# Attention scores and outputs on one core: three 16-column products per block added in PSUM, in place of two products and an addition on VectorE

## The reference

```python
qkv = x @ qkv_w.T + qkv_b
q, k, v = (...)                                   # 12 heads of 16 channels
attn = jnp.einsum('bhid,bhjd->bhij', q, k) * scale
a = jax.nn.softmax(attn, axis=-1)                 # the first layer masks attn before this
out = jnp.einsum('bhij,bhjd->bhid', a, v)
return out @ out_w.T + out_b
```

## Time and profile before

| What | Value |
|---|---|
| Runs before | 509.74, 505.12 and 509.55 us, median 509.55 |
| The profiled execution | 506.86 us, span 505.1 us, mean granted TensorE clock 0.780 |
| PE busy | 344.7 us (68%), 3474 matmuls |
| PEld busy | 257.1 us (51%), 3474 weight loads |
| DVE busy | 412.2 us (82%), 896 instructions |
| ACT busy | 227.3 us (45%), 391 instructions |
| POOL busy | 144.7 us (29%), 194 instructions |

### The profile page before, as it was taken

How to read it: one execution, slowest core, us unless ns; L and a number is a source line. 1 busy time by engine, 2 the same in 40 slices (tenths; PEclk the granted TensorE clock), 3 DMA queues, 4 the chain that set the end, 5 groups by cost and what they waited for, 6 DMA issues and landing times.

```text
span 505.1 us, 8830 instructions
## 1 busy us (share of the span) xinstructions
PE 344.7 (68%) x3474; PEld 257.1 (51%) x3474; DVE 412.2 (82%) x896; ACT 227.3 (45%) x391; POOL 144.7 (29%) x194
## 2 busy tenths in 40 slices
PE   4766649897769899999926000006799268798976
PEld 4665619596646567776702000004359125655955
DVE  3799998998886654887779999998899869776974
ACT  4566383718375796644315660000084122363171
POOL 3535252042430433242042469811301120000000
PEclk9979986959577999999968555555599668578586
DMA  7635000030050002000000000000000000000000
GB/s 275 228 106 228 2 1 1 1 143 1 2 215 1 2 0 95 2 1 1 0 2 1 0 0 0 0 1 0 2 0 1 1 1 1 1 2 1 2 34 31
DMA packets 4235, 17.51 MB, mean 35 GB/s; under 512 B 857, under 2 KB 1762, under 8 KB 3682
## 3 DMA queue, kind: packets, MB, share of 16 engines
q1 hardware_dynamic: 4194, 16.95, 9.2%
HBM read 16.16 MB, written 0.79 MB: 34 GB/s over the span
## 4 chain that ended last, share of the span: by engine, by line
DVE 46%; PE 34%; ACT 8%; issue 6%; POOL 4%; DMA 1%; SPq 0%; DVEq 0%; POOLq 0%; ACTq 0%
PE PS L1527 30%; DVE R L1108 4%; DVE R L1378 3%; DVE R L1380 3%; POOL rstd L511 3%; DVE R L1432 2%; DVE Q L1098 2%; PE PS L1659 2%; DVE R L1001 1%; DVE stats L1011 1%; DMA T<-tok_w 1%; DVE xn L1021 1%; DVE stats L964 1%; POOL ve L508 1%; PE PS L1666 1%
## 5 line engine op out<-in xcount | busy, mean ns | idle before, releaser
L1527 PE MATMUL PS<-late_a,Q 128*128 128x192 f16 x48 | 9.9, 360 | 72.0 <-DVE Q L1435 70.3
L508 POOL TENSOR_SCALAR ve<-mv 128x1 f32<-128x1 f32 x56 | 14.4, 257 | 149.9 <-DVE mv L1012 131.1
L1527 PE MATMUL PS<-Q,R 128*128 128x32 f16 (+3 forms) x1024 | 46.4, 192 | 14.0 <-DVE R L1108 9.7
L1527 PE MATMUL PS<-m,Q 128*128 128x192 f16 (+1 forms) x576 | 51.9, 245 | 2.4 <-DVE Q L1324 2.4
L1527 PEld LDWEIGHTS PS<-Q,R 64*64 64x64 f16 (+1 forms) x1024 | 44.6, 125 | 17.2 <-DVE R L1108 10.2
L1527 PEld LDWEIGHTS PS<-m,Q 128*128 128x128 f16 (+1 forms) x576 | 45.8, 96 | 11.8 <-issue 8.0
L1527 PEld LDWEIGHTS PS<-late_a,Q 128*128 128x128 f16 x48 | 6.2, 139 | 73.8 <-issue 73.4
L1324 DVE TENSOR_TENSOR Q<-Q 128x512 f16<-128x512 f32 x36 | 26.5, 751 | 19.2 <-ACT Q L813 19.0
L1527 PE MATMUL PS<-X_hi,R 128*128 128x512 f16 x144 | 41.2, 392 | 0.0
L808 ACT ACTIVATE Q<-PS,col 128x512 f32<-128x512 f32 x36 | 24.8, 689 | 28.9 <-PE PS L1527 28.8
L1108 DVE TENSOR_SCALAR R<-Q,K 128x1024 f16<-128x1024 f16 x80 | 37.3, 539 | 0.3
(11 more groups left out here) (233 smaller groups left out, 932.3 us busy)
## 6 DMA issues: line engine op xcount, KB each, us to landing
R<-tok_x SPq DMA_DIRECT2D x8, 480.0 KB, 3.6
T<-tok_w SPq DMA_DIRECT2D x6, 480.0 KB, 7.3
T<-late SPq DMA_DIRECT2D x1, 2632.0 KB, 8.7
T<-moe SPq DMA_DIRECT2D x1, 2304.0 KB, 8.8
T<-moe SPq DMA_DIRECT2D x1, 1728.0 KB, 8.0
T<-full SPq DMA_DIRECT2D x1, 1152.0 KB, 5.3
R<-early SPq DMA_DIRECT2D x1, 776.0 KB, 9.8
out<-H SPq DMA_DIRECT2D x4, 192.0 KB, 1.9
```

What stands on the lines that cost most here:

```text
L508: nc.gpsimd.tensor_scalar(ve[:, t:t + 1], mv[:, t, 1:2], EPS, None, ALU.add).then_inc(pool_step, 1)
L1527: return T_.matmul(o, w, x, start=start, stop=stop, skip_group_check=True)
```

## The change

A block's three products now go to the same 16 columns, one after the other, and add in PSUM: high weights by high tokens, high weights by low tokens, low weights by high tokens. VectorE's additions are gone. A fill holds 16 sequences instead of 8, so a stage fills two banks instead of four; within a fill, first all blocks of 128 rows are computed, then all of 64. Scores are copied out of PSUM by ScalarE (two copies of 128x512 in a stage) instead of being written by VectorE. Outputs are split straight from PSUM by ScalarE and VectorE.

```diff
-                for i in range(4 if step in ("st", "ot") else 2):
-                    f.add((step, a, hf, i), by={"st": "st_ready", "pt": "pt_ready", "ot": "os_ready"}.get(step))
+                for i in range(2):
+                    f.add((step, a, hf, i), by={"st": "st_ready", "pt": "pt_ready", "ot": "ot_ready"}.get(step))
...
-                    elif step in ("pt", "ot"):
+                    elif step in ("st", "pt", "ot"):
                         for pr in range(2):
...
+                            name = (step, a, hf, pr)
+                            filled(name)
+                            v = bank(name).rearrange("p (t k n) -> p t k n", t=2, k=2)
+                            if step == "st":
+                                nc.scalar.activation(ST[:, pr], v, ACT.Copy).then_inc(st_ready, 1)
                             else:
-                                act.wait_ge(os_ready, 4 * (2 * a + hf) + 2 * pr + 2)
-                                d, v = O_hi, OS[:, 2 * pr:2 * pr + 2]
...
+                                d = PT[:, 0] if step == "pt" else O_hi
+                                d = d[:, 2 * pr:2 * pr + 2]
+                                nc.scalar.activation(d[:, :, 0], v[:, :, 0], ACT.Copy).then_inc(act_step, 1)
+                                ast[0] += 1
+                                nc.scalar.activation(d[0:CB, :, 1], v[0:CB, :, 1], ACT.Copy).then_inc(hi_ready, 1)
...
-                def two_columns(dst, src):
-                    return V.tensor_reduce(dst, src.rearrange("p (l n) -> p n l", l=2), AX, ALU.add)
-
-                def scores_sum(hf):
-
-                    if 2 * a + hf:
-                        dve.wait_ge(ot_ready, 2 * (2 * a + hf))
-                    for i in range(4):
-                        name = ("st", a, hf, i)
-                        filled(name)
-                        b = bank(name)
-                        two_columns(ST[:, i // 2, i % 2, 0], b[:, 0:2 * P])
-                        two_columns(ST[0:CB, i // 2, i % 2, 1], b[0:CB, 2 * P:4 * P]).then_inc(st_ready, 1)
...
                 def outputs_low(hf):
 
-                    for i in range(4):
-                        name = ("ot", a, hf, i)
-                        filled(name)
-                        b = bank(name)
-                        two_columns(OS[:, i, 0], b[:, 0:2 * P])
-                        two_columns(OS[0:CB, i, 1], b[0:CB, 2 * P:4 * P]).then_inc(os_ready, 1)
                     for pr in range(2):
+                        name = ("ot", a, hf, pr)
                         next_high()
+                        v = bank(name).rearrange("p (t k n) -> p t k n", t=2, k=2)
                         sl = slice(2 * pr, 2 * pr + 2)
-                        V.tensor_tensor(O_lo[:, sl], OS[:, sl, 0], O_hi[:, sl, 0], ALU.subtract)
...
+                        V.tensor_tensor(O_lo[:, sl], v[:, :, 0], O_hi[:, sl, 0], ALU.subtract)
...
-                    for t in range(4):
-                        name = ("st", a, hf, t)
+                    for pr in range(2):
+                        name = ("st", a, hf, pr)
                         free(name)
-                        oa, ob = (bank(name)[:, 2 * P * k:2 * P * (k + 1)].rearrange("p (l n) -> p l n", l=2) for k in range(2))
-                        for s in range(8):
-                            g = 8 * t + s
-                            q, o = slice(16 * g, 16 * g + 16), slice(16 * s, 16 * s + 16)
-                            mm(oa[:, :, o], KAbd[:, 0, g], qa[:, :, q], True, False)
-                            mm(oa[:, 0, o], KAbd[:, 1, g], qa[:, 0, q], False, True)
...
+                        o = bank(name).rearrange("p (t k s n) -> p t k s n", t=2, k=2, s=8)
+                        for kd, qd, k, m in ((KAbd, qa, 0, P), (KVBbd, qb, 1, CB)):
+                            for g in range(16 * pr, 16 * pr + 16):
+                                d, q = o[0:m, g // 8 % 2, k, g % 8], slice(16 * g, 16 * g + 16)
+                                mm(d, kd[0:m, 0, g], qd[0:m, 0, q], True, False)
+                                mm(d, kd[0:m, 0, g], qd[0:m, 1, q], False, False)
+                                last = mm(d, kd[0:m, 1, g], qd[0:m, 0, q], False, True)
                         last.then_inc(psum_filled, 1)
...
-                        pe.wait_ge(st_ready, 4 * (2 * a + hf) + 2 * pr + 2)
+                        pe.wait_ge(st_ready, 2 * (2 * a + hf) + pr + 1)
```

More of the change, by code:

```diff
@@ L434, in build @@
                    "st_ready": st_ready, "v_dve_ready": v_dve_ready, "v_act_ready": v_act_ready, "pt_ready": pt_ready,
[L435 removed]
+                   "ot_ready": ot_ready, "ct_ready": ct_ready, "gelu_ready": gelu_ready,
                    "kvr_ready": kvr_ready, "relu_ready": relu_ready, "tanh_ready": tanh_ready, "hw_ready": hw_ready}
@@ L760, in attention @@
                             nc.scalar.activation(SM[:, pr], SM[:, pr], ACT.Exp).then_inc(exp_ready, 1)
[L761 removed]
+                    elif step in ("st", "pt", "ot"):
                         for pr in range(2):
[L763 to L774 removed]
+                            name = (step, a, hf, pr)
[3 more added lines that the diff above has]
+                                nc.scalar.activation(ST[:, pr], v, ACT.Copy).then_inc(st_ready, 1)
+                            else:
+                                d = PT[:, 0] if step == "pt" else O_hi
[3 more added lines that the diff above has]
+                                nc.scalar.activation(d[0:CB, :, 1], v[0:CB, :, 1], ACT.Copy).then_inc(hi_ready, 1)
+                                hn[0] += 1
                     spare((step, hf))
@@ L1697, in outputs @@
                     pe.wait_ge(v_dve_ready, 4 * (n0 + 1))
-                    for t in range(4):
-                        name = ("ot", a, hf, t)
+                    for pr in range(2):
+                        name = ("ot", a, hf, pr)
                         free(name)
-                        pe.wait_ge(pt_ready, 2 * n0 + t // 2 + 1)
-                        oa, ob = (bank(name)[:, 2 * P * k:2 * P * (k + 1)].rearrange("p (l n) -> p l n", l=2) for k in range(2))
-                        for s in range(8):
-                            g = 8 * t + s
-                            q = o = slice(16 * s, 16 * s + 16)
-                            mm(oa[:, :, o], VA[:, 0, g], PT[:, :, t, 0, q], True, False)
-                            mm(oa[:, 0, o], VA[:, 1, g], PT[:, 0, t, 0, q], False, True)
-                        for s in range(8):
-                            g = 8 * t + s
-                            q = o = slice(16 * s, 16 * s + 16)
-                            mm(ob[0:CB, :, o], VB[0:CB, 0, g], PT[0:CB, :, t, 1, q], True, False)
-                            last = mm(ob[0:CB, 0, o], VB[0:CB, 1, g], PT[0:CB, 0, t, 1, q], False, True)
+                        pe.wait_ge(pt_ready, 2 * n0 + pr + 1)
+                        o = bank(name).rearrange("p (t k s n) -> p t k s n", t=2, k=2, s=8)
+                        for vd, k, m in ((VA, 0, P), (VB, 1, CB)):
+                            for g in range(16 * pr, 16 * pr + 16):
+                                t, q = g // 8, slice(16 * (g % 8), 16 * (g % 8) + 16)
+                                d = o[0:m, t % 2, k, g % 8]
+                                mm(d, vd[0:m, 0, g], PT[0:m, 0, t, k, q], True, False)
+                                mm(d, vd[0:m, 0, g], PT[0:m, 1, t, k, q], False, False)
+                                last = mm(d, vd[0:m, 1, g], PT[0:m, 0, t, k, q], False, True)
                         last.then_inc(psum_filled, 1)
```

13 lines of the change are left out of this document (1 added, 12 removed).

## The result

The changed kernel took 517.2 us (median of 4, 512.96 to 518.25), the kernel before 507.9 us beside it: 1.017 times, 95% interval 1.013 to 1.021. Slower, and within 0.2 us of the forecast. A second comparison gave 514.5 us (4 runs, beside 507.9 us) and 1.014 (1.009 to 1.019), so the 0.2 us are in part luck. The eight times reach from 512.3 to 518.7 us, their middle is 515.5. The loss is 9.2 us in one comparison and 6.6 in the other, the sum said 9.8.

The account below looks back on a forecast made before the run. No engine alone was taken to bound the kernel; each stage's last-ending wait did. Terms 2.3 + 4.3 - 1.6 - 0.6 + 4.8 + 0.6 = +9.8 us on 507.4 gave 517 us, range 509.5 to 522.

Parts of the forecast that it names:

- Price of a product: All eight stages: each third product costs one full weight-load step, 28 or 55 ns at low clock; a stage 8.2 us.
- First stage, +2.3 us: Scores at 76.18: start 1.0 us earlier, but a longer stage and ScalarE's fuller queue delay the outputs by 2.3 us.
- the clock suffers more: Rival: stages at 99.72 and 462.92 begin low, transposes behind 105.04 and 462.92 run low; +14, 521.5 us; 10%.
- the clock rows differ from before: Sign that the forecast is wrong: the stages' clock rows differ from before; the forecast took the clock unchanged, stage by stage.
- Outputs and scores at 99.72 and 105.04, +4.3 us: First attention, TensorE late in both stages: outputs +2.1 us, scores +2.2 us; ScalarE's copies behind a late transfer stay hidden.
- Outputs at 128.15, -1.6 us: First attention's last outputs: longer stage passes beside VectorE's norms; projection starts at 138.2 instead of 139.80, -1.6 us.
- Scores at 426.09, -0.6 us: Last attention's first scores: stage +2.2 us, but the 2.80 us wait for VectorE's addition goes; -0.6 us.
- Outputs and scores at 462.92, +4.8 us: Last attention's middle stages: clock full only at the beginning, 8.1 and 8.2 us against 11.49; +4.8 us.
- Outputs at 490.78, +0.6 us: Last outputs: end 2.2 us later, and the projection begins at 499.0 instead of 498.44; +0.6 us.
- Full clock in longer stages or shared loads: Rival: stages keep 5.9 us and only the gains from waits remain, -7.5, giving 500 us, faster; 7%.
- ScalarE as the bound: Rival: ScalarE's copies behind the late transfer hold the scores at 105.04; +3, 520 us; 4%.
- The return of the clock at its old place: Rival: clock returns as before behind 105.04 and 462.92, speeding the stretches' last 4 to 5 us; +5, 512.5 us; 18%.

Follow-up runs that it names:

- 32 columns: The changed kernel with 32 moving columns in each product in place of 16, the last block of each eight keeping 16: 517.0 us, 1.021.
- four products: The changed kernel with a fourth product in each block, low weights by the low half of the moving operand: 535.1 us, 1.052.
- first profile: The first profiled execution of the changed kernel, nothing else altered: 516.23 us.
- second profile: The changed kernel run again unaltered for a second profiled execution: 514.15 us; median of that comparison 514.5 us.
- pieces ahead: The changed kernel with ScalarE's four spare pieces put back ahead of the first score stage's two score copies: 513.5 us, 1.014.

## Why the prediction was right, step by step

- **Price of a product.** Right: 27 and 53 ns against 28 and 55, 8.12 us a stage against 8.2. That the columns do not set the step is shown by 32 columns, that a third addition costs nothing by the rows of the changed kernel, and that a load is paid each time by four products. Beside it, the prediction put the price by the Trainium skill's formula (TensorE: Matmul & The Clock Gate, LDWEIGHTS) at about 1 us more for the outputs at 99.72; by its own terms, 24 loads of 64 columns at 53 ns in place of 33, it is 0.5 us.
- **First stage, +2.3 us.** The start came as worked out. In the coordinates of before (the first profile runs 0.3 us ahead there, the second 0.5) it is 75.1 in both, against 75.2. ScalarE's first piece behind it came at 96.84 + 0.33 = 97.2, the forecast to a tenth, and at 95.90 + 0.5 = 96.4 in the second profile. That the first agrees so well is luck. In the second profile ScalarE worked without a blank from the score copy on and needed 13.1 us where the sum had 13.7 (0.6 + 4.7 + 8.4); in the first it waited 0.60 us for VectorE in the same stretch, and with the four pieces out of the way (pieces ahead) it came no earlier. The effect on the outputs' start was +4.0 us in the first profile and +1.6 in the second. The mechanism, ScalarE's full queue, holds for the second; in the first the clock stayed low behind the stage and TensorE was late too. The prediction had no price for a low clock at this place: it took the clock as before, and its rival "the clock suffers more" names other stages. It is the sign "the clock rows differ from before", and by the last column of the table it is common with the new form.
- **Outputs and scores at 99.72 and 105.04, +4.3 us.** Interval II: +3.6 in both profiles, and the sum of its own terms was 4.4 (7.5 against 5.3 is 2.2, not 2.1). The stages took 15.75 us, as forecast (7.5 + 8.2); the transposes behind them had the full clock in both profiles, where they were partly low before (granted clock 0.50 until 116.0 us, the transposes from 114.8). A transfer in front of ScalarE's copies was hidden, as costed:

```profile
117.12 0.68 ACT L708 ACTIVATE m<-T 128x576 f16<-128x576 f32 x1 [5.34 <-DMA T<-moe]
...
119.22 0.60 ACT L765 ACTIVATE Q<-PS 128x512 f32<-128x512 f32 x1 [0.36 <-PE PS L1504]
```

- **Outputs at 128.15, -1.6 us.** Interval III: -1.8 in both. Right.
- **Scores at 426.09, -0.6 us.** Interval V: -0.5 and -0.8. Right in size, but reached by two roads. In the second profile the softmax started 0.8 us nearer to the stage and this stayed. In the first the stage ran partly at full clock (7.33 us) and the softmax started 2.1 us nearer:

```profile
444.46 0.55 DVE L1119 TENSOR_SCALAR Q<-PS 128x384 f32<-128x384 f32 x1
```

  and in the kernel before:

```profile
442.06 0.56 DVE L1121 TENSOR_SCALAR Q<-PS 128x384 f32<-128x384 f32 x1 [0.81 <-PE PS L1677]
```

  13.85 us behind the stage's start, 15.97 before (426.09 to 442.06); 1.7 us of it were gone at the outputs (22.52 us on to 466.98 against 20.86 before).
- **Outputs and scores at 462.92, +4.8 us.** Interval VI: +4.6 and +4.2. Right.
- **Outputs at 490.78, +0.6 us.** Interval VII: +0.4 in both. Right.
- **The sum.** 9.8 us forecast; the spans of the two profiles are 9.3 and 7.3 us longer than that of before, the middles of all runs 7.6 apart. The mis-sized terms are the second (0.7 too much) and the first, which is 1.6 or 4.0; the rest is interval IV (-0.9 and +0.8) and what lies ahead of I and behind VII.
- **The rivals.** Full clock in longer stages or shared loads (500 us): excluded by the rows at 0.50 and by four products. The clock suffers more (521.5 us): not at the stages that it named, but behind the first one, and there in one profile of two. ScalarE as the bound (520 us, for its copies behind the late transfer): the transfer was hidden. The return of the clock at its old place (512.5 us): in neither profile for both stretches, though the second profile comes near it behind the first stage (11.0 us behind its start, 9.1 before); three of the eight times (512.3 to 514.2) lie nearer to 512.5 than to 517.

I trusted one number more than it deserved: the sum was made against one execution of before, and its clock taken "as it was, stage by stage". In interval I two executions of the same kernel differ by 2.4 us, along with their clock.

## What to carry over

Where many small blocks go through TensorE, count weight loads, not moving columns: joining two halves in one wider product cost nothing before, and parting them cost 512 loads and 16 us. Look who is late at each stage before taking work from an engine: TensorE waited for the additions in front of three of eight, and with the new form in those alone the kernel came out 2.9 us faster instead of 7.6 slower. With wide loads this choice no longer shows: the new form everywhere, in three stages and in four cannot be told apart. And a block of 64 weight columns is worth loading as 128, with a neighbour beside it whose result nobody reads; it cost a few lines of indexing and turned a loss of 8 us into a gain of 6.

## What I had not expected of the hardware

- A 64x128 load takes half the time of a 64x64 load at the low clock (27 against 53 ns), and 25 against 32 at the full one. The full-clock row, 16 wide loads of the kernel before, in the columns of the earlier trace rows:

```profile
100.14:100.55 0.41, 0.41 (x20) 0.40 (x16) 0.41 (x3) 0.00 (x0) 0.41 (x1) 1.00 0.00 0
```

- With wide loads a step hardly depends on the clock (27 or 25 ns). The kernels' times scatter no less for it (497.92 to 505.17 us in one of them, 505.38 to 509.49 in the kernel before beside it), so the scatter must come from elsewhere; where, is not shown.
- Dense products of this kind do not hold TensorE at its full clock, with 16 columns or with 32: in each of the twelve profiles the granted clock stood at 0.50 at the end of every stage (of the pair, where two run back to back), also where the stage had begun at 1.00. Which property of them does it, no run here separates.
